# First pair of an attention kernel: projections two at a time, high weight halves first, other staging places for the value weights

## The chip, the core and the metric

The kernel runs on one core of a Trainium2 chip. Its engines are TensorE (PE in the profile), VectorE (DVE), ScalarE (ACT), GpSimd (POOL) and the queue of SyncE (SP), from which nearly all transfers are issued. Each engine runs its own list of instructions in order and waits at semaphores for the others. The metric is the time of one execution on the device in microseconds (us), as the median of the runs.

## What is computed

One block over 16 batches of 64 tokens of width 1024, each with a context of 1024 x 1024. Cut to what matters:

```
q1 = fake_quant(layernorm(x));  q2 = fake_quant(ctx)        # 8-bit codes
x  = x + q1 @ q2                                            # cross product, K = 1024
h  = layernorm(x)
q, k, v = split(h @ qkv_w + qkv_b)                          # 1024 -> 3 x 1024, 32 heads of 32
x  = x + softmax(causal(rope(q) @ rope(k).T * scale)) @ v @ out_w + out_b
x  = x + layernorm(x) @ (W + sum of scaled A,B pairs).T + bias
```

## The kernel before

Two batches are one pair, 128 rows, so there are 8 pairs (i = 0 to 7). A pair takes these steps: its context comes in 16 chunks of 128x1024 (8 per batch), ACT turns each into codes (`quantise`, slot c mod 6 of `code`), and PE multiplies it (`chunk`, two products of 512 columns). The chunks of the first batch (0 to 7) and of the second (8 to 15) add up in the same two banks, `X`. DVE adds them to the rows `xa` (`cross_evac(i, b)`), then normalises (`norm2`), PE turns the result (`x_turn`), ACT makes its high half in f16 (`x_high`) and DVE the low one (`x_low`). Six projections of 512 columns follow (`qkv(i, j)`, banks `D[0]` and `D[1]` in turn), each of 24 products: for each of 8 weight tiles high rows by high weights, high rows by low weights, low rows by high weights (`dense`, L1086 to L1088). DVE rotates the first four (`rotate`), PE turns them (`qk_turn`), the scores follow (`scores`), the softmax on DVE (`softmax_in`: maximum and difference; `softmax_out`: sum and quotient) with the exponent on ACT, the turn of its result (`p_turn`), the values (`values`) and the output projection (`project`; in pair 0 `project_whole` in f32 with the raw weights, L1218). DVE takes it up into `xb` (`out_evac`), on top of a base (`out_base`: `xa` plus the output bias).

Cross products of pair i + 1 are done between the steps of pair i. For that `xa` must hold the rows of pair i + 1: `x_shift(i + 1)` on DVE puts them there after `out_base(i)` has read the old ones. For pair 1 these rows are loaded into `xa` by POOL, which waits for `out_base(0)` (`s_cp`), and `x_shift(1)` waits for that load (`s_x`).

The wait that keeps the two halves of a pair apart in the banks `X` is in `chunk` on PE:

```python
                if c == KC:
                    pe.wait_ge(s_ce, 2 * i + 1)
                pe.wait_ge(s_u8, CHUNKS * i + c + 1)
```

Pair 0 is also when the weights arrive: 24 tiles of 128x1024 in f32 for the projections (0 to 7 query, 8 to 15 key, 16 to 23 value) and 8 for the output (24 to 31). Each lands in a staging place, ACT writes its high half (`weight_hi(j)`, semaphore `s_whi`) and DVE its low half (`weight_lo(j)`, `s_wlo`), and the staging place is free again. Places: query weights lie where the value weights will be (`v_stage`), key weights in the output weights' room (`o_stage`), value weights 16 to 20 in `v_stage` again and 21 to 23 in parts of `at`. Since value weights are staged in the places of value weights, their high half may be written only when an older low half is done.

The order of pair 0 is written out by hand on each engine in `first_pair`, of pair 1 in `next_pair(1, ...)`, which also makes the halves of weights 25 to 31; pairs 2 to 6 are a loop. SP issues in its written order as well: chunks of pair 0, weights 0 to 16, then chunks of pair 1 and weights 17 to 27 in turn. Chunks of pair 1 and later use three slots: the two of `raw` and `lnt`.

## Time and profile before

| | us |
|---|---|
| median of 3 runs | 654.68 (653.92 to 655.34) |
| profiled execution, its time | 654.89 |
| its span | 653.2 |
| PE busy | 610.1 (93%) |
| DVE busy | 447.6 (69%) |
| ACT busy | 297.6 (46%) |

The span is what the instructions cover; 1.7 us of the execution's time lie around it. A busy PE is one that works or whose products are in the pipeline. A timeline row gives start, duration, engine, line, operation, output and inputs, and in brackets the idle time before it with what ended it. A duration has a tail that overlaps the next instruction of the engine, so a step in a chain is better read from start to start. PEclk, the granted clock, is 1.00 at 2.4 GHz and 0.50 at 1.2 GHz.

### The profile page before, as it was taken

What the parts mean: (1) busy time and instruction counts of PE and PEld (TensorE: products, weight loads), DVE (VectorE), ACT (ScalarE), POOL (GpSimd) and SP (SyncE); (2) the same over time, 40 slices, a digit from 0 to 9 for tenths busy, and PEclk for the clock granted to TensorE, in tenths of its full rate; (3) what the DMA queues carried; (4) which work ended last, traced back from release to release, by engine and by line L of the source; (5) the groups of instructions that cost most, each with busy time, mean ns of one, the idle gap of its engine ahead of it and who ended that gap; (6) DMA issues with size and microseconds to landing.
All of it is one profiled execution on the core that took longest, in us unless ns stands there. A gap on an engine that the chain in (4) does not pass through costs nothing.

```text
span 653.2 us, 12686 instructions
## 1 busy us (share of the span) xinstructions
PE 610.1 (93%) x4864; PEld 308.5 (47%) x4864; DVE 447.6 (69%) x895; ACT 297.6 (46%) x374; POOL 11.1 (2%) x20
## 2 busy tenths in 40 slices
PE   1659979998999999999999999999999999899997
PEld 0224444454545555554555455555545554445453
DVE  6599956877755863885487558737674568866761
ACT  5986955773455355455544653544331242201010
POOL 3000000000000000000000000000000000000000
PEclk9769989999999999999999999999999999999999
DMA  8999983861175136416631761363230043113221
GB/s 322 386 388 398 346 314 147 283 231 66 59 265 193 66 144 215 156 64 229 211 115 53 263 221 64 121 232 129 96 131 31 3 149 142 48 66 128 73 89 48
DMA packets 38494, 109.17 MB, mean 167 GB/s; under 512 B 4026, under 2 KB 4282, under 8 KB 38464
## 3 DMA queue, kind: packets, MB, share of 16 engines
q1 hardware_dynamic: 36688, 104.35, 44.7%
q0 software_dynamic: 1344, 4.23, 1.7%
q8 instruction: 20, 0.33, 0.2%
q10 hardware_dynamic: 432, 0.18, 0.1%
q14 instruction: 10, 0.08, 0.0%
HBM read 100.35 MB, written 8.39 MB: 166 GB/s over the span
## 4 chain that ended last, share of the span: by engine, by line
PE 77%; DVE 11%; DMA 5%; issue 3%; SPq 2%; ACT 2%; DVEq 0%; ACTq 0%
PE dense L1086 15%; PE dense L1087 15%; PE dense L1088 14%; PE cross L1108 6%; PE turn L1076 6%; PE dense L1202 4%; PE dense L1203 4%; PE dense L1204 4%; DVE wq L754 3%; PE score L1163 2%; DMA lnt<-in_ctx 2%; SPq L535 2%; DMA wq<-in_ctx 2%; PE score L1189 2%; PE dense L1095 1%
## 5 line engine op out<-in xcount | busy, mean ns | idle before, releaser
L1086 PE MATMUL dense<-wq,xn_h 128*128 128x512 f16 x448 | 170.9, 381 | 5.6 <-DVE at L786 2.1
L1087 PE MATMUL dense<-wq,xn_h 128*128 128x512 f16 x448 | 170.8, 381 | 0.0
L1088 PE MATMUL dense<-wq,xn_l 128*128 128x512 f16 x448 | 170.5, 381 | 0.0
L310 ACT ACTIVATE code<-raw,cst,qc 128x1024 uint8<-128x1024 f32 x77 | 93.8, 1236 | 9.8 <-DMA raw<-in_ctx 8.6
L1108 PE MATMUL cross<-code,q1t 128*128 128x512 f16 x256 | 75.5, 402 | 4.5 <-DVE xa L761 3.5
L1086 PEld LDWEIGHTS dense<-wq,xn_h 128*128 128x128 f16 x448 | 43.9, 98 | 54.3 <-issue 5.9
L1088 PEld LDWEIGHTS dense<-wq,xn_l 128*128 128x128 f16 x448 | 44.0, 98 | 53.4 <-issue 1.0
L1087 PEld LDWEIGHTS dense<-wq,xn_h 128*128 128x128 f16 x448 | 44.0, 98 | 43.0 <-issue 0.5
L783 DVE TENSOR_REDUCE smx<-score 128x8 f32<-128x512 f32 x32 | 22.0, 686 | 49.8 <-PE score L1163 49.8
L310 ACT ACTIVATE code<-lnt,cst,qc 128x1024 uint8<-128x1024 f32 x35 | 43.3, 1238 | 27.4 <-DMA lnt<-in_ctx 20.4
L326 ACT ACTIVATE at<-turn 128x512 f32<-128x512 f32 x32 | 19.0, 595 | 76.2 <-PE turn L1076 76.2
L771 DVE TENSOR_TENSOR rope<-dense,cst 128x512 f32<-128x512 f32 x32 | 22.0, 688 | 36.4 <-PE dense L1088 36.4
L1108 PEld LDWEIGHTS cross<-code,q1t 128*128 128x128 f16 x256 | 25.8, 102 | 40.0 <-issue 7.7
L1202 PE MATMUL dense<-wo,rope 128*128 128x512 f16 x112 | 42.5, 380 | 0.0
L1203 PE MATMUL dense<-wo,rope 128*128 128x512 f16 x112 | 42.4, 379 | 0.0
L1204 PE MATMUL dense<-wo,rope 128*128 128x512 f16 x112 | 42.4, 379 | 0.0
L334 ACT ACTIVATE at<-at 128x512 f32<-128x512 f32 x32 | 20.0, 626 | 40.8 <-DVE at L786 40.8
L760 DVE SCALAR_TENSOR_TENSOR xa<-cross,qc,xa 64x1024 f32<-64x1024 f32 x16 | 20.4, 1274 | 15.6 <-PE cross L1108 15.4
L340 ACT ACTIVATE at<-turn 128x512 f32<-128x512 f32 x32 | 19.0, 595 | 21.6 <-PE turn L1076 21.6
L1086 PE MATMUL dense<-wq,q1t 128*128 128x512 f16 x64 | 24.3, 379 | 0.0
L1087 PE MATMUL dense<-wq,q1t 128*128 128x512 f16 x64 | 24.3, 379 | 0.0
L1088 PE MATMUL dense<-wq,q1t 128*128 128x512 f16 x64 | 24.3, 379 | 0.0
(146 smaller groups left out, 870.2 us busy)
## 6 DMA issues: line engine op xcount, KB each, us to landing
raw<-in_ctx SPq DMA_DIRECT2D x77, 512.0 KB, 4.3
lnt<-in_ctx SPq DMA_DIRECT2D x35, 512.0 KB, 4.3
wq<-in_qkv_w SPq DMA_DIRECT2D x13, 512.0 KB, 11.8
wo<-in_ctx SPq DMA_DIRECT2D x8, 512.0 KB, 8.7
wq<-in_ctx SPq DMA_DIRECT2D x8, 512.0 KB, 11.7
wo<-in_qkv_w SPq DMA_DIRECT2D x8, 512.0 KB, 12.8
x_scratch<-xb SPq DMA_DIRECT2D x8, 512.0 KB, 3.0
wq<-x_scratch SPq DMA_DIRECT2D x8, 512.0 KB, 3.6
```

The costliest lines, as they stand in the source:

```text
L310: act.activation(low_bytes, src, ACT.Identity, scale=qc[:, 1:2], bias=z2).then_inc(s_u8, 1)
L760: link(dve.scalar_tensor_tensor(xa[rows, :], XX[0:SEQ, :], qc[0:SEQ, 2:3], xa[rows, :], ALU.mult, ALU.add))
L771: dve.tensor_tensor(t1, src, cosb, ALU.mult)
L783: link(dve.tensor_reduce(smx[:, g % 2, :], s3, AX.X, ALU.max))
L1076: ins = pe.transpose(bank[:, k * P:(k + 1) * P], src[:, c:c + P], ident)
L1086: pe.matmul(bank[:, :], a_h[:, k, :], w_hi, start=(k == 0 and not started), stop=False)
L1087: pe.matmul(bank[:, :], a_h[:, k, :], w_lo, start=False, stop=False)
L1088: ins = pe.matmul(bank[:, :], a_l[:, k, :], w_hi, start=False, stop=(k == KC - 1))
L1108: ins = pe.matmul(X[n][:, :], lhs, code[:, c % RING, n * NT:(n + 1) * NT], start=(kc == 0), stop=(kc == KC - 1))
L1202: pe.matmul(D[n][:, :], c_h[:, k, :], wo_h[:, k, cols], start=(k == 0), stop=False)
L1203: pe.matmul(D[n][:, :], c_h[:, k, :], wo_l[:, k, cols], start=False, stop=False)
L1204: ins = pe.matmul(D[n][:, :], c_l[:, k, :], wo_h[:, k, cols], start=False, stop=(k == KC - 1))
```

## The change

- **PE, pair 0.** The six projections run in three sets of two banks. Of each set the products with the high weight halves run first for both banks (`high`), then those with the low halves (`low`). `high` waits for `s_whi`, `low` for `s_wlo`. For the first tiles of the first set the products of the high rows run ahead of those of the low rows. The bias products of the first set are ahead of `x_turn`. Chunks of pair 1 start in the low products of the last set, and chunks 7 and 8 stand between the first values and the output projection.
- **Staging.** Value weights 16 to 23 lie in `at`, in both slots of `raw`, in `lnt`, in `at` twice, in `spare` and in the first place of `o_stage`, all outside the places of value weights.
- **SP.** All 24 projection weights and output weights 24 to 27 are issued before the first chunk of pair 1. Chunks 0 to 2 of pair 1 wait for the low halves 17 to 19, which free their slots. Weights 28 to 30 follow chunks 13 to 15.
- **ACT and DVE, pair 0.** Their orders are written anew: ACT makes the high halves up to 23 before any code of pair 1, DVE has `out_base(0)`, `x_shift(1)` and both `cross_evac(1, ...)` behind more of the softmax. The last chunk of pair 0 is coded half on ACT and half on DVE (`last_codes`), and the norm of pair 0 is written in two halves, so that its turn can start on the first.
- **Pair 1.** Low half 31 moves on DVE behind two `softmax_in`.
- ACT's wait before it writes a slot of `code` names, for the first four chunks of a pair, a later product than before.

```diff
@@ staging, SP @@
-            if j < 2 * KC + 5:
-                return v_stage[j - 2 * KC + 3]
             if j < W_QKV:
-                return at_stage[:, j - 2 * KC - 5, :, :]
+                return value_stage[j - 2 * KC]
...
-            for c in range(7):
+            for j in range(W_QKV, W_QKV + 4):
+                load_weight(j)
+            for c in range(13):
                 load_chunk(1, c)
-                load_weight(17 + c)
...
@@ ACT, quantise @@
-                if above(CHUNKS * i + c - RING + 1):
-                    act.wait_ge(s_cmm, CHUNKS * i + c - RING + 1)
+                taken = CHUNKS * i + c - (CHUNKS % RING - 1 if c < CHUNKS % RING else RING - 1)
+                if above(taken):
+                    act.wait_ge(s_cmm, taken)
...
@@ DVE, first_pair @@
-                w(2, 9)
+                w(1, 9)
                 rotate(0, 0)
-                w(9, 13)
                 rotate(0, 1)
-                w(13, 16)
-                out_base(0)
+                w(9, 16)
                 rotate(0, 2)
-                w(16, 20)
                 rotate(0, 3)
-                w(20, 24)
+                w(16, 21)
                 softmax_in(0, 0)
                 softmax_in(0, 1)
-                x_shift(1)
+                w(21, 24)
                 softmax_out(0, 0)
                 softmax_out(0, 1)
-                cross_evac(1, 0)
+                out_base(0)
                 softmax_in(0, 2)
                 softmax_in(0, 3)
+                x_shift(1)
                 softmax_out(0, 2)
                 softmax_out(0, 3)
+                cross_evac(1, 0)
                 cross_evac(1, 1)
...
@@ DVE, next_pair @@
                 cross_evac(i + 1, 0)
-                w(31)
                 if more:
                     row_stats(i + 2, x_early)
                 softmax_in(i, 2)
                 softmax_in(i, 3)
+                w(31)
...
@@ DVE, codes of the last chunk of pair 0 @@
             cross_evac(0, 0)
+            last_codes()
             cross_evac(0, 1)
...
@@ PE, first_pair @@
+                low(2, tiles_due(KC))
+                low(3)
+                started(4)
+                high(4, range(KC), both, high_due(2 * KC), {3: [at(turned, 0, 0), at(qk_turn, 0, 2)], 7: [at(turned, 0, 1), at(qk_turn, 0, 3)]})
+                started(5)
+                high(5, range(KC), both, None, {2: [at(scores, 0, 0)]})
+                low(4, tiles_due(2 * KC), {3: [at(c, 0)], 4: [at(scores, 0, 1), at(c, 1)], 5: [at(c, 2)]})
+                low(5, None, {0: [at(turned, 0, 2), at(p_turn, 0, 0)], 5: [at(p_turn, 0, 1)]})
+                c(3, 4, 5, 6)
                 values_due(0, 0)
-                c(10)
                 values(0, 0)
-                project_whole(0, 0, {0: [at(evacuated, 0, 0), at(p_turn, 0, 2)], 1: [at(c, 11)], 2: [at(evacuated, 0, 1), at(p_turn, 0, 3)], 3: [at(c, 12, 13)]})
-                c(14, 15)
-                project_whole(1, 0, {2: [at(values_due, 0, 1)], 3: [at(values, 0, 1)]})
+                c(7, 8)
+                project_whole(0, 0, {0: [at(c, 9)], 1: [at(evacuated, 0, 0), at(p_turn, 0, 2)], 2: [at(c, 10)], 3: [at(evacuated, 0, 1), at(p_turn, 0, 3)]})
+                project_whole(1, 0, {0: [at(c, 11)], 1: [at(c, 12)], 2: [at(values_due, 0, 1)], 3: [at(values, 0, 1)]})
+                c(13, 14, 15)
```

How the instructions stand shows best at three places; the semaphores that each waits for are in brackets. First DVE in pair 0, around the first `cross_evac` of pair 1 (L760 and L761 before, L763 and L764 after) and the row shift (L738, L730); `smx` and `ssum` are softmax inputs and outputs. Before:

```order
L783 TENSOR_REDUCE smx<-score 128x8 [waits s_sc]
L786 TENSOR_TENSOR at<-score,smx 128x512 [waits s_dv]
L738 TENSOR_SCALAR xa<-xa,rs 128x1024 [waits s_x]
L792 TENSOR_REDUCE ssum<-at 128x8 [waits s_exp,s_xs]
L793 RECIPROCAL ssum<-ssum 128x8 [waits s_dv]
L794 TENSOR_TENSOR at<-at,ssum 128x512 [waits s_dv]
L792 TENSOR_REDUCE ssum<-at 128x8 [waits s_exp]
L793 RECIPROCAL ssum<-ssum 128x8 [waits s_dv]
L794 TENSOR_TENSOR at<-at,ssum 128x512 [waits s_dv]
L760 SCALAR_TENSOR_TENSOR xa<-cross,qc,xa 64x1024 [waits s_cmm]
L761 SCALAR_TENSOR_TENSOR xa<-cross,qc,xa 64x1024 [waits s_dv]
L783 TENSOR_REDUCE smx<-score 128x8 [waits s_sc]
```

After, behind the output base (L719) and the first of two softmax inputs:

```order
L786 TENSOR_REDUCE smx<-score 128x8 [waits s_sc]
L789 TENSOR_TENSOR at<-score,smx 128x512 [waits s_pt,s_dv]
L730 TENSOR_SCALAR xa<-xa,rs 128x1024 [waits s_x]
L795 TENSOR_REDUCE ssum<-at 128x8 [waits s_exp,s_xs]
L796 RECIPROCAL ssum<-ssum 128x8 [waits s_dv]
L797 TENSOR_TENSOR at<-at,ssum 128x512 [waits s_dv]
L795 TENSOR_REDUCE ssum<-at 128x8 [waits s_exp]
L796 RECIPROCAL ssum<-ssum 128x8 [waits s_dv]
L797 TENSOR_TENSOR at<-at,ssum 128x512 [waits s_dv]
L763 SCALAR_TENSOR_TENSOR xa<-cross,qc,xa 64x1024 [waits s_cmm]
L764 SCALAR_TENSOR_TENSOR xa<-cross,qc,xa 64x1024 [waits s_dv]
```

The evacuation of chunks 0 to 7 moved from ahead of the second half's softmax to behind all of it, and the shift with its wait `s_x` went with it.

PE in pair 0 around chunk 8 of pair 1 (`cross` with the wait `s_ce`). Before, in the last products of the sixth projection (L1086 to L1088), with the values of the first half (L1189) and the first product of the output projection (L1218) behind:

```order
L1088 MATMUL dense<-wq,xn_l 128x512
L1108 MATMUL cross<-code,q1t 128x512 [waits s_u8,s_ce]
L1108 MATMUL cross<-code,q1t 128x512
L1086 MATMUL dense<-wq,xn_h 128x512
L1087 MATMUL dense<-wq,xn_h 128x512
L1088 MATMUL dense<-wq,xn_l 128x512
L1108 MATMUL cross<-code,q1t 128x512 [waits s_u8]
L1108 MATMUL cross<-code,q1t 128x512
L1108 MATMUL cross<-code,q1t 128x512 [waits s_sub,s_u8,s_pte,s_v]
L1108 MATMUL cross<-code,q1t 128x512
L1189 MATMUL score<-at 32x64 x32
L1218 MATMUL dense<-wo,rope 128x512 [waits s_w24,s_cl,s_v]
```

After, behind the values of the first half (L1193), with the output projection (L1222) and a turn of the softmax (L1078) behind:

```order
L1193 MATMUL score<-at 32x64 [waits s_sub,s_pte,s_v]
L1193 MATMUL score<-at 32x64 x31
L1112 MATMUL cross<-code,q1t 128x512 [waits s_u8]
L1112 MATMUL cross<-code,q1t 128x512
L1112 MATMUL cross<-code,q1t 128x512 [waits s_u8,s_ce]
L1112 MATMUL cross<-code,q1t 128x512
L1222 MATMUL dense<-wo,rope 128x512 [waits s_w24,s_cl,s_v]
L1112 MATMUL cross<-code,q1t 128x512 [waits s_u8]
L1112 MATMUL cross<-code,q1t 128x512
L1222 MATMUL dense<-wo,rope 128x512 [waits s_w25]
L1078 MATMUL turn<-cst,at 128x128 [waits s_p,s_pte]
L1078 MATMUL turn<-cst,at 128x128 x3
```

Chunk 8 stood ahead of the first values and among projection products; now it stands behind them, and the output projection behind it.

DVE in pair 1, from its `cross_evac` on (L760 and L761 before): low half 31 (`wo<-spare`) and the statistics of the rows after next (from L688). Before:

```order
L760 SCALAR_TENSOR_TENSOR xa<-cross,qc,xa 64x1024 [waits s_cmm]
L761 SCALAR_TENSOR_TENSOR xa<-cross,qc,xa 64x1024 [waits s_dv]
L754 SCALAR_TENSOR_TENSOR wo<-spare,wo 128x1024 [waits s_whi]
L688 BN_STATS st<-at 128x6 [waits s_x]
L689 BN_STATS st<-at 128x6
L690 MEMSET nw 128x1 [waits s_dv]
L691 BN_AGGR mv<-st 128x2
```

After, from the end of those statistics (L702, L703) on, with the low half at L757:

```order
L702 TENSOR_SCALAR ab<-nw,qc 128x1 [waits s_dv]
L703 SCALAR_TENSOR_TENSOR ab<-mv,ab,cst 128x1 [waits s_dv]
L786 TENSOR_REDUCE smx<-score 128x8 [waits s_sc,s_dv]
L789 TENSOR_TENSOR at<-score,smx 128x512 [waits s_pt,s_dv]
L786 TENSOR_REDUCE smx<-score 128x8 [waits s_sc]
L789 TENSOR_TENSOR at<-score,smx 128x512 [waits s_pt,s_dv]
L757 SCALAR_TENSOR_TENSOR wo<-spare,wo 128x1024 [waits s_whi]
L795 TENSOR_REDUCE ssum<-at 128x8 [waits s_exp]
```

The low half went from ahead of the statistics to behind both softmax inputs.

## Rows read from the trace of the kernel before

**Rows 1.** Waits of PE from 180 us on: us in total, times, longest.

```profile
PE cross L1243 <- DVE wq L815: 3.2, 3, 2.2
```

**Rows 2.** Timeline of PE: start us, us, what [idle before it].

```profile
95.05 2.05 PE L1218 MATMUL dense<-wo,rope 128*128 128x512 f32 x2 [4.63 <-issue]
...
106.56 0.86 PE L1189 MATMUL score<-at 64*32 64x64 f32 x64
...
116.42 0.38 PE L1095 MATMUL dense<-bias_t,pick 128*128 128x512 f16 x1 [0.25 <-DVE xb L809]
...
162.69 0.49 PE L1086 MATMUL dense<-wq,xn_h 128*128 128x512 f16 x1 [2.11 <-DVE at L786]
...
180.58 0.38 PE L1095 MATMUL dense<-bias_t,pick 128*128 128x512 f16 x1
...
240.90 0.38 PE L1095 MATMUL dense<-bias_t,pick 128*128 128x512 f16 x1
```

**Rows 3.** Timeline of DVE, pair 0.

```profile
37.26 0.81 DVE L744 TENSOR_SCALAR lnt<-xa,mv,nw 128x1024 f32<-128x1024 f32 x1
...
61.45 1.22 DVE L727 TENSOR_TENSOR xb<-xa,outb 128x1024 f32<-128x1024 f32 x1
62.59 0.68 DVE L771 TENSOR_TENSOR rope<-dense,cst 128x512 f32<-128x512 f32 x1
...
63.52 0.41 DVE L773 TENSOR_TENSOR rope<-dense,cst 128x256 f32<-128x256 f32 x1
...
78.92 0.74 DVE L738 TENSOR_SCALAR xa<-xa,rs 128x1024 f32<-128x1024 f32 x1
79.70 0.69 DVE L792 TENSOR_REDUCE ssum<-at 128x8 f32<-128x512 f32 x1
...
82.82 1.27 DVE L760 SCALAR_TENSOR_TENSOR xa<-cross,qc,xa 64x1024 f32<-64x1024 f32 x1
...
85.45 0.69 DVE L783 TENSOR_REDUCE smx<-score 128x8 f32<-128x512 f32 x1
...
87.50 0.69 DVE L786 TENSOR_TENSOR at<-score,smx 128x512 f32<-128x512 f32 x1
...
103.23 1.28 DVE L760 SCALAR_TENSOR_TENSOR xa<-cross,qc,xa 64x1024 f32<-64x1024 f32 x1 [8.75 <-PE cross L1108]
```

**Rows 4.** Timeline of DVE, pair 1.

```profile
154.52 1.23 DVE L754 SCALAR_TENSOR_TENSOR wo<-spare,wo 128x1024 f16<-128x1024 f32 x1 [3.01 <-ACT wo L293]
...
159.80 0.69 DVE L783 TENSOR_REDUCE smx<-score 128x8 f32<-128x512 f32 x1
```

**Rows 5.** Windows: us, busy PE, PEld, DVE, ACT, POOL, PEclk, DMA share, GB/s.

```profile
95.00:96.00 1.00, 0.95 (x1) 0.50 (x2) 0.00 (x0) 0.00 (x0) 0.00 (x0) 0.50 0.98 344
...
163.00:164.00 1.00, 1.00 (x10) 0.16 (x11) 0.93 (x3) 0.20 (x1) 0.00 (x0) 0.50 0.00 0
```

**Rows 6.** Timeline of ACT, pair 0.

```profile
27.73 2.55 ACT L310 ACTIVATE code<-wq,cst,qc 128x1024 uint8<-128x1024 f32 x2 [0.21 <-DMA wq<-in_ctx]
...
101.14 1.23 ACT L310 ACTIVATE code<-raw,cst,qc 128x1024 uint8<-128x1024 f32 x1
107.45 0.66 ACT L353 ACTIVATE rope<-score 128x256 f32<-128x256 f32 x2 [5.08 <-PE score L1189]
...
108.94 2.37 ACT L310 ACTIVATE code<-raw,cst,qc 128x1024 uint8<-128x1024 f32 x2
```

**Rows 7.** Timeline of POOL, pair 0.

```profile
62.97 0.54 POOL L669 DMA_DIRECT2D xa<-in_x  x1 [24.05 <-DVE xb L727]
```

**Rows 8.** DMA issues, 60 to 100 and 180 to 240 us: KB each, us to landing.

```profile
xa<-in_x POOLq DMA_DIRECT2D x1, 512.0 KB, 6.9
...
at<-in_x POOLq DMA_DIRECT2D x1, 512.0 KB, 5.4
```

**Rows 9.** Line L551, which loads chunks, up to 180 us.

```profile
DMA to landing us min/median/max: 3.0/4.1/6.4
```

**Rows 10.** The page's first line.

```profile
span 653.2 us, 12686 instructions
```

More of the change, by code:

```diff
@@ L505, in _ @@
             a_high(1, 1)
-            for j in range(5):
+            for j in range(6):
                 weight_hi(j)
@@ L540, in load_chunk @@
                         sp.wait_ge(s_u8, CHUNKS * i + c - 2)
-                    elif c == 2:
-                        sp.wait_ge(s_xt, 2)
+                    else:
+                        sp.wait_ge(s_wlo, 2 * KC + 2 + c)
                     sp.dma_start(slots[n], ctx_v[i, c // KC, c % KC, :, :]).then_inc(s_ctx0[c], 16)
@@ L739, in x_shift, with last_codes @@
                 dve.wait_ge(s_xs, i + 1)
+            def last_codes():
+                c = CHUNKS - 1
+                dve.wait_ge(s_ctx0[c], 16)
+                dve.wait_ge(s_cmm, c - RING + 1)
+                low_bytes = code[:, c % RING, :].bitcast(U8T).rearrange("p (a n b) -> p a n b", a=2, b=2)[:, 1, :, 0]
+                dve.tensor_scalar(low_bytes, chunk0_stage(c)[:, 1, :], qc[:, 1:2], z2, ALU.mult, ALU.add).then_inc(s_u8half, 1)
             def norm2(i):
@@ L743, in norm2 @@
                 mean_rstd(xa[:, :], XSC)
-                dve.tensor_scalar(lnt[:, :], xa[:, :], mv[:, 0:1], nw[:, 0:1], ALU.subtract, ALU.mult).then_inc(s_xn, 1)
+                if isinstance(i, int) and i == 0:
+                    dve.tensor_scalar(lnt[:, 0:NT], xa[:, 0:NT], mv[:, 0:1], nw[:, 0:1], ALU.subtract, ALU.mult).then_inc(s_xnhalf, 1)
+                    dve.tensor_scalar(lnt[:, NT:DM], xa[:, NT:DM], mv[:, 0:1], nw[:, 0:1], ALU.subtract, ALU.mult).then_inc(s_xn, 1)
+                else:
+                    dve.tensor_scalar(lnt[:, :], xa[:, :], mv[:, 0:1], nw[:, 0:1], ALU.subtract, ALU.mult).then_inc(s_xn, 1)
             def x_low(i, e):
@@ L965, in _ @@
             cross_evac(0, 0)
+            last_codes()
             cross_evac(0, 1)
             norm2(0)
-            for j in range(2):
-                weight_lo(j)
+            weight_lo(0)
             x_low(0, 0)
@@ L1105, in chunk @@
                 pe.wait_ge(s_u8, CHUNKS * i + c + 1)
+                if isinstance(i, int) and i == 0 and c == CHUNKS - 1:
+                    pe.wait_ge(s_u8half, 1)
                 lhs = q1t[:, kc, b, :, :].rearrange("p h t -> p (h t)")
@@ L1224, in x_turn @@
             def x_turn(i, first=False):
-                pe.wait_ge(s_xn, i + 1)
+                if first:
+                    pe.wait_ge(s_xnhalf, 1)
+                else:
+                    pe.wait_ge(s_xn, i + 1)
                 for e in range(2):
@@ L1266, in evacuated, with started, high, low @@
                 pe.wait_ge(s_pte, 4 * i + g + 1)
+            def started(j):
+                if j > 1:
+                    pe.wait_ge(s_rt, j - 1)
+                bias(D[j % 2], order(0)[j])
+            def high(j, ks, rows, due=None, between={}):
+                n = order(0)[j]
+                for k in ks:
+                    if due:
+                        due(k)
+                    for a in rows:
+                        pe.matmul(D[j % 2][:, :], a[:, k, :], wq_h[:, k, n * NT:(n + 1) * NT], start=False, stop=False)
+                    for step in between.get(k, ()):
+                        step()
+            def low(j, due=None, between={}):
+                n = order(0)[j]
+                for k in range(KC):
+                    if due:
+                        due(k)
+                    ins = pe.matmul(D[j % 2][:, :], xn_h[:, k, :], wq_l[:, k, n * NT:(n + 1) * NT], start=False, stop=(k == KC - 1))
+                    if k == KC - 1:
+                        ins.then_inc(s_qkv, 1)
+                    for step in between.get(k, ()):
+                        step()
+            def high_due(start):
+                return lambda k: pe.wait_ge(s_whi, start + k + 1)
             def first_pair():
@@ new lines, in first_pair @@
+                both = (xn_h, xn_l)
+                high(0, range(5), (xn_h,), rows_high)
+                high(0, range(5), (xn_l,), rows_low)
+                high(0, range(5, KC), both, rows_high)
+                high(1, range(KC), both)
+                low(0, tiles_due(0))
+                low(1)
+                started(2)
+                high(2, range(KC), both, high_due(KC), {7: [at(qk_turn, 0, 0)]})
+                started(3)
+                high(3, range(KC), both, None, {7: [at(qk_turn, 0, 1)]})
```

94 lines of the change are left out of this document (42 added, 52 removed).

## The prediction

> **What bounds the kernel now.** I read the waits of TensorE (PE) first. From 180 us to the end they add up to 4 us [rows 1]: the loop over the pairs keeps PE full, and one pair takes 60.32 us from bias to bias (180.58 to 240.90) [rows 2]. Nothing in the change touches that loop, so its time moves only with the moment at which the loop begins. The two pairs ahead of it do have holes. Pair 0 holds PE up for 4.63 us before the output projection (95.05), and pair 1 takes 64.16 us from 116.42 to 180.58, 3.84 more than a pair of the loop [rows 2]. The reader is to see two chains there. In pair 0 VectorE (DVE) is full from 37.26 to 82.82 with the low weight halves, the rotations and the softmaxes; then the end of the block is set by the last chunk of context of pair 1: its evacuation starts on DVE at 103.23, and PE begins pair 1 13.19 us later [rows 2, 3]. In pair 1 DVE waits 3.01 us for ScalarE (ACT) to give the high half of weight 31 (154.52), so its softmax of the second half starts at 159.80 and PE waits 2.11 us until 162.69 [rows 2, 4]. PE then runs at half clock [rows 5]: the granted clock is 0.50 at 163 to 164, the lower of its levels (1.2 of 2.4 GHz).
>
> **The start.** The last chunk of codes is split, half on ACT, half on DVE. Two whole ones take 2.55 us on ACT, one alone 1.23 [rows 6], and half is some 0.6: a gain of 0.6, less about 0.05 for the norm written in two halves (0.81 whole, at 37.26 [rows 3]). So 0.55. The new instruction on DVE stands where DVE waits for the same chunk anyway, so it is free. Bounds: 0 (DVE's half takes as long as the whole) to 0.65.
>
> **The projections two at a time.** PE no longer waits for low halves before it uses high ones. But DVE's work stays: 24 low halves, 4 rotations, 2 low row halves, 2 softmax inputs, 2 outputs. DVE is the chain here, so I sum its time by difference. The second softmax output ends at 82.82 now (the next instruction's start) [rows 3]. Taken out ahead of it are the output base (1.14 us, from 61.45 to 62.59) and the row shift (0.78 from 78.92 to 79.70) [rows 3]; the start gives 0.55. I add 0.5 for new small waits (for the rows' high halves, for low products behind the last low half of a set): 82.82 - 1.14 - 0.78 - 0.55 + 0.5 = 80.9. Bounds 80.4 and 82. PE then has one turn and two products left and is done with the projections at about 82. Weight transfers now come in one row, so ACT's high halves keep ahead of DVE; SP's queue issues all 24 before the first chunk of pair 1, whose slot holds value weight 17 until its low half is made. That is 12.7 us before DVE's 80.9 (three low halves, two softmax inputs, three low halves, two outputs), at 68.2. The first chunk's codes then come at about 73 instead of 57, but PE asks for them only at 75. That costs nothing by itself.
>
> At one place a rule speaks against pairing. Here DVE frees a bank while PE runs the eight low products of the other one. The Trainium skill (Perfetto Trace Analysis, Optimizing Tensor Performance, Matmuls) says that independent groups should rotate through different banks so that emptying one overlaps the next group's products; two groups that end together overlap less. By that rule alone two rotations would stand open; by the program they are covered. That rule is priced as a rival below.
>
> **What is late next: chunk 8 of pair 1.** This is the term that decides. Chunks 0 to 7 and 8 to 15 of a pair go to the same banks, so chunk 8 waits until DVE has evacuated chunks 0 to 7 (its `s_ce` wait in PE's order). Before, that evacuation ran at 82.82, ahead of the second half's softmax [rows 3], and PE came to chunk 8 later. After, it is behind the output base, two softmax inputs, the row shift and two softmax outputs. And the shift reads rows that POOL loads into `xa`, issued when the output base is done. So:
> - output base 80.9 to 82.05; POOL issues 0.35 us after its end (61.45 + 1.22 to 62.97 [rows 3, 7]): 82.4.
> - landing: 6.9 us for this load now, on full transfer engines; 5.4 for the like load of pair 2; the shortest chunk load takes 3.0 [rows 8, 9]. I take 5.4, since few chunks are in flight then: 87.8. DVE has come to the shift at 84.7 (two softmax inputs, 2.65: 85.45 to 87.50 + 0.69, less the overlap with what follows [rows 3]) and idles 3.1 us.
> - shift 0.78, two softmax outputs 3.12 (79.70 to 82.82), evacuation 2.63 (82.82 to 85.45) [rows 3]: 94.3. Chunk 8 runs at 94.4.
>
> PE has nothing else. ACT gives the codes of chunks 5 and 6 behind its last copy of the projections (82.6 + 2.37 = 85.0), so the values of the first half end at 86.3; copy (0.55), codes of chunk 7 (1.23) and two products (0.43) come to 88.5. Then chunk 8 heads PE's queue, and the whole output projection stands behind it. So PE idles about 6 us, where it idled 4.63 before. From chunk 8 to the end of the second half's values PE has the same work as now from 95.05: four products of the first projection and four of the second, two turns, five chunks, one set of values. That took 106.56 + 0.86 - 95.05 = 12.4 us, the half-clock stretch after the hole in it (granted clock 0.50 at 95 to 96) [rows 2, 5]. Since the hole is longer now, I take the same 12.4: 106.8. At full clock it would be 10.9.
>
> Then comes a piece that wasn't in series before: ACT's order puts the context copy (0.66 long, 0.55 in series) and chunks 14 and 15 (2.37) behind those values, and from the last code to the evacuation it takes 0.86 (101.14 + 1.23 to 103.23) [rows 3, 6]. 106.8 + 0.55 + 2.37 + 0.86 = 110.6 against 103.23: 7.4 us later. Behind it stands the same DVE chain of 13.19 us (evacuation, norm, next rows' statistics, low rows, output). PE's remaining work, one half projection of 3.5, the turn and another of 3.5, fits under it even if half of it runs at half clock. So pair 1 starts 7.4 us later. Bounds: the load lands in 3.0 (-2.4) or 6.9 (+1.5), the clock costs 0 (-1.5) or twice (+1.5).
>
> **Pair 1.** Low half 31 moves on DVE from ahead of the statistics to behind the two softmax inputs. The statistics then start right after the evacuation, at 151.5 in this trace's time (154.52 - 3.01) and take the same 4.1, and the inputs then wait for nothing but the scores, which PE ends at about 155.9; now they start at 159.80 [rows 4]. They end at 158.6, before PE asks at 160.4. Hole and half clock go; the pair then takes what a loop pair takes: -3.84, of which I count 3.7, since PE's turn of the next rows comes only 0.2 us after DVE has them. Bounds -3.0 and -3.84. The new ring waits (`s_cmm`) of ACT are met long before; the other pairs are unchanged.
>
> **Sum.** On the profiled execution (654.89 us, its span 653.2 [rows 10]): +7.4 - 3.7 = +3.7, 658.6. The median of the runs is 654.68, 0.2 below it, so the forecast is 658.4.
>
> **The rivals.**
> - Same: the rows land in 3.0 us and PE keeps its full clock. 7.4 - 2.4 - 1.5 - 3.7 = -0.2: 654.5. For it: transfers are thin at that point. Against it: both 512 KB loads by POOL read here took 5.4 or more, and after a hole of 4.63 the clock was halved [rows 2, 5, 8]. Chance 0.13, taken to be within 0.2% (1.3 us, about what a measurement of this kernel can tell from no change).
> - Faster: the change does what it says, because the evacuation is not what chunk 8 waits for (DVE far earlier than I sum). Then ACT's codes bind: chunk 8's at 89.3 (copy after the values at 86.9, two chunks 2.37), 10.9 of PE and 3.8 of ACT and PE, 104.0: +0.8 - 3.7 = -2.9, 651.8. It decides once the evacuation ends before 89.3, 5.0 earlier than I get. Against it: DVE has no idle time to lose. Chance 0.09.
> - Open rotations: the time from first to last reading of a bank, 1.34 of a rotation (62.59 to 63.52 + 0.41 [rows 3]), comes into the chain once (ahead of the scores) and finds 0.15 of slack: +1.2, 659.6. Chance 0.12. It is the rule above as a mechanism.
> - Pair 1 keeps its hole, since ACT gives weight 31 late or the row turn becomes the wait: +7.4, 662.1. Chance 0.08.
> - My case: 0.58.
>
> **How the numbers follow.** The range takes in the load's and the clock's bounds: 654.6 to 661.2. What's left out is most of the faster case and the last one. Faster by over 0.2% 0.09, within 0.2% 0.13, slower 0.78.
>
> **What would show it.** Right: the first evacuation of pair 1 on DVE at about 91.7 with a wait for a transfer of about 3 us before the shift; PE idle before chunk 8 for about 6 us; granted clock 0.5 behind it; last evacuation at about 110.6; pair 1 from bias to bias 60.4 to 60.5. Wrong: chunk 8 runs before 90, or the wait before it names ACT's codes; pair 1 still over 63; projections that end after 84, since then DVE's chain is missummed.

## The result: slower by 0.8%, and where the time stands

The changed kernel takes 660.26 us (median of four runs, 659.31 to 661.05) against 654.30 for the kernel before, measured beside it: a ratio of 1.0079, 95% interval 1.0052 to 1.0107. The forecast was 658.4, range 654.6 to 661.2. The profiled execution took 659.62 us, and its page begins (before: [rows 10]):

```profile
span 658.0 us, 12691 instructions
```

The waits of PE from 180 us on are the old one and nothing else [rows 1], so the loop over the pairs is unchanged:

```profile
PE cross L1252 <- DVE wq L818: 3.2, 3, 2.2
```

The timeline of PE (start us, us, what, idle before it) shows both halves of the result; the rows answer to [rows 2]:

```profile
90.47 1.03 PE L1112 MATMUL cross<-code,q1t 128*128 128x512 f16 x2 [1.88 <-ACT code L313]
95.48 1.03 PE L1112 MATMUL cross<-code,q1t 128*128 128x512 f16 x2 [3.98 <-DVE xa L764]
96.31 1.91 PE L1222 MATMUL dense<-wo,rope 128*128 128x512 f32 x2
...
108.20 0.86 PE L1193 MATMUL score<-at 64*32 64x64 f32 x64
...
125.89 0.38 PE L1097 MATMUL dense<-bias_t,pick 128*128 128x512 f16 x1 [1.50 <-DVE xb L812]
...
186.30 0.38 PE L1097 MATMUL dense<-bias_t,pick 128*128 128x512 f16 x1
...
246.62 0.38 PE L1097 MATMUL dense<-bias_t,pick 128*128 128x512 f16 x1
```

Pair 1 begins at 125.89 instead of 116.42, 9.47 later. It then takes 60.41 us (to 186.30) instead of 64.16, 3.75 less, practically a pair of the loop (60.32). So the loop begins 5.72 later. The span grew by 4.8 only: from pair 3's bias to the end it is 411.4 us here and 412.3 before, of which 0.8 is a wait at the start of the feed-forward part that this trace lacks. That tail is not touched by any kernel of this study, and it spread from 411.4 to 414.1 over the thirteen traces. In the six with a tail of 413.0 or more the granted clock fell, once, between 550 and 575 us (to 0.66 to 0.82 in the lowest stretch of 5 us); in the seven with 412.5 or less it stayed 1.00 from 240 us on. So I compare traces at the biases, and whole kernels by medians.

What PE waited for at 95.48 stands on DVE; the rows answer to [rows 3], and the pairing's first half did what it was to do (DVE's softmax output ends at 82.25, and no low half is waited for on DVE):

```profile
37.61 0.55 DVE L744 TENSOR_SCALAR lnt<-xa,mv,nw 128x512 f32<-128x512 f32 x1
38.08 0.54 DVE L745 TENSOR_SCALAR lnt<-xa,mv,nw 128x512 f32<-128x512 f32 x1
...
82.25 1.22 DVE L719 TENSOR_TENSOR xb<-xa,outb 128x1024 f32<-128x1024 f32 x1
...
88.92 0.75 DVE L730 TENSOR_SCALAR xa<-xa,rs 128x1024 f32<-128x1024 f32 x1 [2.80 <-DMA xa<-in_x]
...
92.83 1.27 DVE L763 SCALAR_TENSOR_TENSOR xa<-cross,qc,xa 64x1024 f32<-64x1024 f32 x1
...
112.71 1.28 DVE L763 SCALAR_TENSOR_TENSOR xa<-cross,qc,xa 64x1024 f32<-64x1024 f32 x1 [17.29 <-PE cross L1112]
```

And POOL, which issues the load (before: 62.97 [rows 7]):

```profile
83.76 0.53 POOL L661 DMA_DIRECT2D xa<-in_x  x1 [44.31 <-DVE xb L719]
```

Two engines' orders meet here. On ACT's timeline the codes of pair 1 wait for their context five times, 8.7 us in all; the two longest waits are shown, before the first chunk (whose codes came at 55.65 before) and before chunk 10. The last two chunks stand behind the copy of the second half's values, as forecast (before: [rows 6]):

```profile
73.28 1.24 ACT L313 ACTIVATE code<-raw,cst,qc 128x1024 uint8<-128x1024 f32 x1 [3.19 <-DMA raw<-in_ctx]
...
96.35 1.24 ACT L313 ACTIVATE code<-raw,cst,qc 128x1024 uint8<-128x1024 f32 x1 [3.10 <-DMA raw<-in_ctx]
...
109.10 0.66 ACT L356 ACTIVATE rope<-score 128x256 f32<-128x256 f32 x2 [2.23 <-PE score L1193]
109.64 1.24 ACT L313 ACTIVATE code<-lnt,cst,qc 128x1024 uint8<-128x1024 f32 x1
110.78 1.24 ACT L313 ACTIVATE code<-raw,cst,qc 128x1024 uint8<-128x1024 f32 x1
```

The windows (us, busy PE, PEld, DVE, ACT, POOL, PEclk, DMA share, GB/s) show what the two holes of PE did to its clock (before: [rows 5]):

```profile
85.00:90.00 5.00, 2.32 (x68) 1.17 (x68) 2.13 (x4) 4.22 (x7) 0.00 (x0) 0.73 0.83 292
90.00:95.00 5.00, 1.03 (x2) 0.13 (x2) 4.83 (x8) 2.89 (x3) 0.53 (x1) 0.50 0.85 301
95.00:100.00 5.00, 4.52 (x8) 1.98 (x9) 0.42 (x1) 2.37 (x2) 0.00 (x0) 0.50 0.73 269
100.00:105.00 5.00, 5.00 (x19) 2.50 (x18) 0.00 (x0) 1.59 (x3) 0.00 (x0) 0.90 0.92 333
```

### The profile page after: what moved, and what is told of

It is laid out like the page before. It is cut to its first block, busy times and chain, and to the rows that moved or that the text cites. A ratio compares the mean times of both kernels' runs of the same rounds, so it can differ in the third digit from the quotient of the medians.

```text
span 658.0 us, 12691 instructions
## 1 busy us (share of the span) xinstructions
PE 610.8 (93%) x4864; PEld 307.9 (47%) x4864; DVE 448.2 (68%) x897; ACT 298.3 (45%) x374; POOL 11.1 (2%) x20
## 4 chain that ended last, share of the span: by engine, by line
PE 81%; DVE 12%; DMA 3%; SPq 2%; issue 1%; ACT 1%; DVEq 0%; ACTq 0%
PE dense L1088 15%; PE dense L1090 15%; PE dense L1089 15%; PE cross L1112 7%; PE turn L1078 6%; DVE wq L757 4%; PE dense L1206 4%; PE dense L1207 4%; PE dense L1208 4%; PE score L1167 3%; SPq L525 2%; DMA wq<-in_ctx 2%; PE score L1193 2%; PE dense L1097 1%; PE dense L1222 1%
## 5 line engine op out<-in xcount | busy, mean ns | idle before, releaser
L1088 PE MATMUL dense<-wq,xn_h 128*128 128x512 f16 x400 | 151.8, 380 | 0.0
L1090 PE MATMUL dense<-wq,xn_l 128*128 128x512 f16 x400 | 151.6, 379 | 0.0
L1089 PE MATMUL dense<-wq,xn_h 128*128 128x512 f16 x400 | 151.6, 379 | 0.0
L1112 PE MATMUL cross<-code,q1t 128*128 128x512 f16 x256 | 77.5, 407 | 14.6 <-DVE xa L764 7.4
L1090 PEld LDWEIGHTS dense<-wq,xn_l 128*128 128x128 f16 x400 | 39.1, 98 | 47.2
L1088 PEld LDWEIGHTS dense<-wq,xn_h 128*128 128x128 f16 x400 | 39.1, 98 | 39.7 <-issue 0.6
L1089 PEld LDWEIGHTS dense<-wq,xn_h 128*128 128x128 f16 x400 | 39.1, 98 | 38.9
L1206 PE MATMUL dense<-wo,rope 128*128 128x512 f16 x112 | 42.5, 380 | 0.0
L763 DVE SCALAR_TENSOR_TENSOR xa<-cross,qc,xa 64x1024 f32<-64x1024 f32 x16 | 20.4, 1273 | 18.4 <-PE cross L1112 18.3
L1078 PE MATMUL turn<-cst,lnt 128*128 128x128 f32 x128 | 17.6, 283 | 9.8 <-DVE lnt L744 6.0
L1088 PE MATMUL dense<-wq,q1t 128*128 128x512 f16 x64 | 24.3, 379 | 0.0
L1089 PE MATMUL dense<-wq,q1t 128*128 128x512 f16 x64 | 24.3, 379 | 0.0
```

Of the source, the lines that this page charges most:

```text
L1078: ins = pe.transpose(bank[:, k * P:(k + 1) * P], src[:, c:c + P], ident)
L1088: pe.matmul(bank[:, :], a_h[:, k, :], w_hi, start=(k == 0 and not started), stop=False)
L1089: pe.matmul(bank[:, :], a_h[:, k, :], w_lo, start=False, stop=False)
L1090: ins = pe.matmul(bank[:, :], a_l[:, k, :], w_hi, start=False, stop=(k == KC - 1))
L1112: ins = pe.matmul(X[n][:, :], lhs, code[:, c % RING, n * NT:(n + 1) * NT], start=(kc == 0), stop=(kc == KC - 1))
L1206: pe.matmul(D[n][:, :], c_h[:, k, :], wo_h[:, k, cols], start=(k == 0), stop=False)
```

## The experiments

My theory after the result: the loss is made in pair 0, by chunk 8 of pair 1 standing ahead of the projection while the evacuation of `xa` waits for a load; the gain is made in pair 1, by low half 31 alone. The main rival for the loss was the supply of codes (ACT's order, or the context loads, whose slots now hold value weights until DVE has split them).

The profiled executions differ in the moment at which the last chunk of pair 0 lands, from 28.91 to 30.86 us, though no edit touches the loads up to it. Where two traces are compared, that part of a difference is named.

**Low half 31.** First the gain by itself: the kernel before with this edit and nothing else.

```diff
                 cross_evac(i + 1, 0)
-                w(31)
                 if more:
                     row_stats(i + 2, x_early)
                 softmax_in(i, 2)
                 softmax_in(i, 3)
+                w(31)
```

> The kernel before with one edit of the change: in pair 1 low half 31 stands on DVE behind two softmax inputs. Theory: DVE's statistics start 4 us earlier, PE's hole of 2.11 us in pair 1 and the half clock behind it go, pair 1 takes 60.3 to 60.5 us from bias to bias in place of 64.16, and the kernel 3.7 us less than before (-0.57%). Rival: pair 1 got shorter in the changed kernel only because its start lay otherwise against the transfers; then this edit alone gives 0 to 1 us.

Measured: 651.56 us (12 runs) against 655.52, ratio 0.9949 (0.9930 to 0.9968), -3.3 us by the ratio and -4.0 by the medians. Pair 1 is 60.44 us long there:

```profile
116.24 0.38 PE L1095 MATMUL dense<-bias_t,pick 128*128 128x512 f16 x1 [0.24 <-DVE xb L809]
...
176.68 0.38 PE L1095 MATMUL dense<-bias_t,pick 128*128 128x512 f16 x1
```

The same edit backwards, on the changed kernel:

> The changed kernel with that one edit undone: low half 31 ahead of the statistics again. Theory: pair 1 takes about 64.1 us again, the kernel 3.7 us more than the changed one, so some 9.3 more than before (+1.4%). Rival: as the changed kernel, since its weight 31 lands at another moment.

Measured: 662.90 (6 runs), ratio 1.0116 (1.0089 to 1.0144), 2.4 us over the changed kernel's 1.0079, less than the 3.7 expected; the two intervals touch, so the trace decides. Pair 1 is 64.0 us long again (124.56 to 188.56), and the old wait is back in PE's list of waits:

```profile
PE dense L1088 <- DVE at L789: 2.1, 1, 2.1
```

So the 3.6 to 3.7 us of pair 1 come from this one line and don't depend on the rest. The first of the two beats both kernels.

**The load into `xa`.** The output base moves ahead of low halves 16 to 20, so that POOL issues the load early.

```diff
                 rotate(0, 3)
+                out_base(0)
                 w(16, 21)
...
                 softmax_out(0, 1)
-                out_base(0)
                 softmax_in(0, 2)
```

> The changed kernel with the output base of pair 0 earlier on DVE, ahead of low halves 16 to 20, so that the load of the next rows is issued some 15 us earlier. DVE's wait of 2.80 us before the row shift goes in any case. If that load is what makes chunk 8 of pair 1 late, chunk 8 runs 2.8 us earlier and the kernel takes 2.8 less than the changed one. My theory after its trace: the evacuation can't start before the products of chunk 7 (90.47 + 1.03), whose codes hang on ACT's chain behind the first half's softmax, and that chain gets 1.14 us longer by the base: chunk 8 only 0.2 to 1.5 us earlier, the kernel 0 to 1.5 less than the changed one.

Measured: 660.25 (6 runs), ratio 1.0074 (1.0048 to 1.0099): no gain. On DVE's timeline the shift no longer waits, and the next instruction does, for ACT:

```profile
85.59 0.74 DVE L730 TENSOR_SCALAR xa<-xa,rs 128x1024 f32<-128x1024 f32 x1
88.63 0.69 DVE L795 TENSOR_REDUCE ssum<-at 128x8 f32<-128x512 f32 x1 [2.30 <-ACT at L337]
...
91.99 1.28 DVE L763 SCALAR_TENSOR_TENSOR xa<-cross,qc,xa 64x1024 f32<-64x1024 f32 x1
```

The exponents stand behind the codes of chunks 5 and 6 in ACT's order. The load's wait was real, but another stood right behind it, and the evacuation came only 0.8 earlier (91.99 for 92.83), 0.5 of it because the last chunk of pair 0 landed that much earlier. What was left was lost again behind the last evacuation, which came at 112.01 for 112.71. PE then idled 3.75 us in both traces, but here its turn and half projection behind that hole ran at half clock, and pair 1 began at 126.06 for 125.89:

```profile
119.16 1.97 PE L1078 MATMUL turn<-cst,lnt 128*128 128x128 f32 x8 [3.75 <-DVE lnt L747]
```

**Chunk 8 behind the projection's first half.** On the changed kernel, PE's order only:

```diff
-                c(7, 8)
-                project_whole(0, 0, {0: [at(c, 9)], 1: [at(evacuated, 0, 0), at(p_turn, 0, 2)], 2: [at(c, 10)], 3: [at(evacuated, 0, 1), at(p_turn, 0, 3)]})
-                project_whole(1, 0, {0: [at(c, 11)], 1: [at(c, 12)], 2: [at(values_due, 0, 1)], 3: [at(values, 0, 1)]})
+                c(7)
+                project_whole(0, 0, {1: [at(evacuated, 0, 0), at(p_turn, 0, 2)], 3: [at(evacuated, 0, 1), at(p_turn, 0, 3), at(c, 8, 9)]})
+                project_whole(1, 0, {0: [at(c, 10, 11)], 1: [at(c, 12)], 2: [at(values_due, 0, 1)], 3: [at(values, 0, 1)]})
```

> The changed kernel with only PE's order changed: the first half of the first output projection stands ahead of chunks 8 and 9, which come behind it with 10 and 11. Theory (chunk 8 at the head of PE's queue holds up work that doesn't need it): PE's wait for the evacuation, 3.98 us, vanishes behind the projection, the half clock is paid under it, the values of the second half end 5 to 6 us earlier than at 109.06, and the kernel takes about 5.5 less than the changed one, so about as long as before. Rival (the codes of chunks 10 to 12, whose transfers and ring are late since the slots held weights, bind): less than 2 us less, with waits of PE for ACT's codes in the place.

Measured: 657.76 (12 runs), ratio 1.0032 (1.0012 to 1.0053), half of what I expected. The wait for DVE is gone, and the last evacuation comes at 110.49, 2.2 earlier, 0.5 of that from the start. All that PE still waits for there is codes, 7.8 us against 6.2 in the changed kernel:

```profile
PE cross L1112 <- ACT code L313: 7.8, 7, 2.5
```

But all but 1.9 us of these waits lie ahead of the projection (93.60). From there to the end of the second half's values (106.84) PE waited for nothing; it was slow, at half clock until about 98.4:

```profile
90.00:95.00 5.00, 3.12 (x68) 1.79 (x51) 3.54 (x6) 4.04 (x5) 0.09 (x1) 0.50 0.84 298
95.00:100.00 5.00, 5.00 (x13) 2.42 (x12) 1.41 (x2) 2.11 (x2) 0.00 (x0) 0.66 0.80 261
```

So this run doesn't show by itself that the supply of codes was the limit. The next one, at full clock, does.

Both edits together:

> The changed kernel with both earlier edits together: the output base ahead of the low halves 16 to 20 (so the load into xa starts early), and chunk 8 behind the first projection tile. Theory now: what holds the pair back is the supply of codes for chunks 8 to 15 (each load waits for its slot, each code for the scalar engine), so the base's place matters no more than before: within 0.7 of the kernel with chunk 8 later alone (657.8), 657.1 to 658.5. Rival: the load into xa is the second chain and was only covered by the first: then its wait of 2.2 us goes as well, 655.6.

Measured: 658.79 (4 runs), ratio 1.0066 (1.0040 to 1.0092), nothing gained over chunk 8 alone: the intervals of the two overlap, and counted from DVE's first low half, pair 1 begins 1.7 us earlier than in the changed kernel with chunk 8 alone and 1.4 earlier here. This trace is the clearest one. PE's clock is 1.00 from 75 to 105, the projection starts at 92.19, the second half's values end at 104.7, 4.4 us sooner than in the changed kernel. Still the last evacuation is at 111.29. On ACT's timeline the last codes are what is late:

```profile
103.33 1.24 ACT L313 ACTIVATE code<-raw,cst,qc 128x1024 uint8<-128x1024 f32 x1 [1.82 <-DMA raw<-in_ctx]
104.72 0.66 ACT L356 ACTIVATE rope<-score 128x256 f32<-128x256 f32 x2
106.30 1.24 ACT L313 ACTIVATE code<-lnt,cst,qc 128x1024 uint8<-128x1024 f32 x1 [0.93 <-DMA lnt<-in_ctx]
108.92 1.24 ACT L313 ACTIVATE code<-raw,cst,qc 128x1024 uint8<-128x1024 f32 x1 [1.38 <-DMA raw<-in_ctx]
```

From the first (75.26) to the last (108.92), fifteen intervals take 33.66 us, 2.24 for each chunk: three slots, each refilled only when its codes are made. A chunk's codes take ACT 1.24. From 66 to 116 us ACT sat idle for context 16.1 us in all, 5.2 of it before the first codes, 8.5 between the first and the last, and 2.5 before those of pair 2:

```profile
its engine sat idle before it (us, times) until:
  DMA raw<-in_ctx: 14.9, 9
  DMA lnt<-in_ctx: 1.2, 2
```

**The supply of context taken away.** Two kernels make pair 1's codes from a tile that has long been in place, so pair 1's output is wrong; all instructions and loads stay. Not shown are waits on SP and DVE that keep a place from being written before its last loads have landed.

```diff
                     if isinstance(i, int) and i == 1:
-                        act.wait_ge(s_ctx0[c], 32)
+                        src = outb[:, :].rearrange("p (a n) -> p a n", a=2)
+                        act.wait_ge(s_outb, 16)
...
                     if c >= 3:
-                        sp.wait_ge(s_u8, CHUNKS * i + c - 2)
+                        sp.wait_ge(s_ctx0[c - 3], 32)
```

On the kernel with both edits:

> The same edit of the codes' source (pair 1's codes are made from the output bias tile, so pair 1's output is wrong), on the kernel with the output base early and chunk 8 later. Theory: what is left there is the supply of context chunks, whose first codes start at 75.3 us and whose last are made at 108.9, 2.24 us for each of fifteen, at slots that the value weights held till then. With the data at hand the last evacuation comes at about 105.0 and not 111.3 (projection from 90.0, 11.2 us to the end of the second half's values, two chunks of codes and a chunk's product), so 658.8 - 6.3 = 652.5, 651.5 to 653.8. Rival (the order of the instructions on the scalar engine, which is unchanged, holds the last codes back): within 1 us of 658.8.

Measured: 655.09 (10 runs), ratio 1.0013 (1.0004 to 1.0023), against 1.0066: 0.5%, 3.5 us where I expected 6.3. In the trace the last evacuation is at 105.04, the 105.0 of the sum, and pair 1 begins at 118.24 and not 124.45:

```profile
105.04 1.28 DVE L768 SCALAR_TENSOR_TENSOR xa<-cross,qc,xa 64x1024 f32<-64x1024 f32 x1 [11.70 <-PE cross L1117]
```

0.8 of those 6.2 us is the start: the last chunk of pair 0 landed at 28.99 and not 29.78. So the supply is worth 5.4 at pair 1, with the clock 1.00 in both traces from 75 to 105. 1.6 are taken back in the tail (413.0 against 411.4), where this trace has the fall of the clock and the other has not. Most of what is left between traces and medians is that the traced execution here took 1.4 less than the median of its kernel (653.67), the other one 0.5 less. And on the changed kernel itself:

> The changed kernel, with ScalarE making pair 1's sixteen chunks of codes from the output bias tile (128x1024 f32, long in place) in place of the context that is loaded: the codes of pair 1 are wrong, and so is the output of pair 1; all the loads are still made, each behind the one before it in its slot. This takes the wait for the context out of the scalar engine's order and leaves every instruction. Theory: two chains run side by side in the changed kernel, the codes and the load into xa; with the codes at hand the second is left alone. The load still lands at 88.9, the first evacuation stays at 92.8, chunk 8 at 95.5 and the last evacuation at 112.0 to 112.7: 659.5 to 660.3. Rival (the supply of codes alone sets the end): 3 us or more are gained, 657 or less.

Measured: 661.76 (4 runs), ratio 1.0106 (1.0085 to 1.0127): no gain, perhaps a loss. With the codes at hand the transfer engines were busier (share 0.98 from 85 to 90, for 0.83), and the load into `xa`, issued at 83.04, landed only at 91.1, after 8 us:

```profile
91.14 0.75 DVE L733 TENSOR_SCALAR xa<-xa,rs 128x1024 f32<-128x1024 f32 x1 [5.75 <-DMA xa<-in_x]
```

PE then waited 8.06 us for the evacuation. So this edit made the other chain longer, by the 3 us that the load took more (8.1 for 5.1), and pair 1 began at 126.93. As an estimate from these rows, without that delay it would have begun at about 123.9, or 124.7 if the start had been the changed kernel's. Against the changed kernel's 125.89, and with the start evened out, the load's chain alone taken away gives 1.4 us, the supply alone about 1.2, and both together 6.8. The two chains stand side by side, and each hides most of what the other is worth.

**Where the supply is lost.** Value weights 16 and 17 take the first two slots, so the loads of chunks 0 and 1 wait for one low half fewer (on the kernel with both edits):

```diff
-        value_stage = [at_stage[:, 1, :, :]] + [s.rearrange("p (a n) -> p a n", a=2) for s in slots] + [at_stage[:, 0, :, :], at_stage[:, 2, :, :],
+        value_stage = [s.rearrange("p (a n) -> p a n", a=2) for s in slots[:2]] + [at_stage[:, 1, :, :], slots[2].rearrange("p (a n) -> p a n", a=2)] + [at_stage[:, 0, :, :], at_stage[:, 2, :, :],
...
-                        sp.wait_ge(s_wlo, 2 * KC + 2 + c)
+                        sp.wait_ge(s_wlo, 2 * KC + (1, 2, 4)[c])
```

> As the run with the base early and chunk 8 later, and value weights 16 and 17 in the first two chunk slots (18 in the A^T stage, 19 in the third slot as before), so that the loads of chunks 0 and 1 of pair 1 wait for one low half fewer each. Theory (late chunk loads hold the codes back): the first codes, 73.3 to 74.7 us so far, start some 1.15 us earlier, the refills behind them too, and the kernel gains 0.8 to 1.2. Rival (the scalar engine's order or the DMA queue's rate holds them back): the first codes come earlier and the last evacuation doesn't, within 0.3 of the other run.

Measured: 658.48 (8 runs, 655.31 to 659.41), ratio 1.0050 (1.0029 to 1.0070) against 1.0066 (1.0040 to 1.0092). In the trace the first codes come at 73.16 (75.26) and the last evacuation at 108.58 (111.29); the whole trace is 0.9 earlier from the start, so 1.2 and 1.8 are left. In the trace that is the direction and the size, but the intervals of the times overlap, so this run by itself decides nothing.

**The start.** The changed kernel with whole codes of chunk 15 and whole normalised rows:

> The changed kernel with the split of chunk 15's codes and of the first normalised rows undone (both whole again, as in the kernel before); all else as changed. My forecast's term: the start was 0.55 us earlier by these splits, so undoing them gives 660.3 + 0.55 = 660.8. What the trace after says instead: chunk 15 landed at 29.82 against 29.03 before, its 512-wide codes took 0.82 and not 0.6, and the first low half began at 38.53 against 38.0, so the splits gave nothing that can be seen; then the time stays 660.3 within 0.4, or falls a little, to 659.9.

Measured: 661.98 (6 runs), ratio 1.0105 (1.0084 to 1.0125), where the changed kernel had 1.0079 (1.0052 to 1.0107). The direction is that of a worth of the splits, but the intervals overlap. In this trace the last chunk landed at 30.86, a microsecond later than in the changed kernel's, and PE multiplied it at half clock; a single pair of traces says little here.

Counted from that landing the traces agree. Of the four kernels without the splits, the three that don't have that half clock make ACT's first high part of the rows 10.26 to 10.27 us behind it and start DVE's first low half 8.94 to 8.96 behind it; eight of the nine kernels with the splits take 9.54 to 9.56 and 8.71 to 8.72. So the splits give the rows' high part 0.7 us and DVE 0.25.

**Towards a faster kernel.** The kernel before with low half 31 moved still idles 3.95 us before the projection, since ACT has two exponents, an evacuation and two chunks of codes ahead of the context copy. Only ACT's order changes:

```diff
-                q(11)
                 exponent(0, 2)
-                q(12)
+                q(11)
                 exponent(0, 3)
-                v_evac(0, 1)
-                q(13)
                 c_whole(0)
+                q(12)
+                v_evac(0, 1)
                 p_evac(0, 2)
-                q(14)
+                q(13)
                 p_evac(0, 3)
-                q(15)
+                q(14)
+                q(15)
                 c_whole(1)
```

> The kernel before, with low half 31 moved behind the two softmax inputs (as in the run with that part alone) and ScalarE's order in the first pair's second half changed: exponents 2 and 3 around codes 11, then at once the context rows of the first half, and codes 12 to 15 between the later evacuations. In the run with low half 31 alone, the values of the first half end at 90.7 and ScalarE turns to them only at 93.9, since two exponents, an evacuation and two chunks of codes stand ahead; TensorE is idle 3.95 us there. Theory: the context rows run at 90.75, the projection starts at 91.4 and not 94.6, all that follows moves with it: 651.6 - 3.2 = 648.4. Rival: the last evacuation follows the codes of chunk 15, whose loads and codes (1.24 us each, five of them) don't come earlier: 650.5 to 651.6.

Measured: 647.47 (6 runs) against 654.57 (expected: 648.4), ratio 0.9898 (0.9875 to 0.9921), with the next one the fastest of the study. PE's timeline has the hole cut to 0.80, and its clock is 1.00 from 90 to 100:

```profile
92.13 1.10 PE L1218 MATMUL dense<-wo,rope 128*128 128x512 f32 x2 [0.80 <-issue]
...
113.02 0.38 PE L1095 MATMUL dense<-bias_t,pick 128*128 128x512 f16 x1 [0.24 <-DVE xb L809]
```

With the changed kernel's start added (the splits, and low half 1 behind the first rows' low part):

> The kernel before with three edits: low half 31 behind the two softmax inputs, ScalarE's order of the first pair's second half as in the run with that order, and, taken from the changed kernel, the split of chunk 15's codes and of the first normalised rows over two engines and two pieces, with one low half and not two ahead of the first rows' low part. Over the run with the order (647.5): the first rows' high part came at 38.45 to 39.4 us (mean 38.9 of six) in the kernels with the split, and at 39.3 to 41.5 (mean 40.2 of four) in those without: -0.5 to -1.3, so 646.2 to 647.0. Rival (the low halves or weights that follow are late instead, so the first projections wait): no gain, 647.5.

Measured: 648.01 (4 runs), ratio 0.9900 (0.9883 to 0.9916): the rival, no gain. The rows are there at 39.21 (40.23 without, 0.3 of it the landing), but pair 1 begins at 112.97 (113.02): PE's waits for low halves grew from 2.3 to 3.4 us.

```profile
PE dense L1101 <- DVE wq L769: 3.4, 9, 0.7
```

In the old order each projection still follows DVE, tile by tile, and DVE gets no further by it: its third low half starts at 42.5 in both traces.

## Why the prediction was right, point by point

**Start, -0.55.** Within its bounds, and too large: 0.25. The low halves began 0.5 later than before (38.53 for 37.99), but chunk 15 had landed 0.8 later. Before (the chain, then DVE's timeline), and after:

```profile
29.03 1.25 ACT code L310
37.99 1.22 DVE L754 SCALAR_TENSOR_TENSOR wq<-wq 128x1024 f16<-128x1024 f32 x1
```

```profile
29.82 0.55 DVE L738 TENSOR_SCALAR code<-wq,qc,cst 128x512 uint8<-128x512 f32 x1 [5.77 <-DMA wq<-in_ctx]
38.53 1.22 DVE L757 SCALAR_TENSOR_TENSOR wq<-wq 128x1024 f16<-128x1024 f32 x1
```

ACT's half took 0.82 and not 0.6, and the norm in two halves 0.92 (37.61 to 38.53) for 0.73 whole, so it cost 0.2 and not 0.05.

**DVE's sum, 80.9.** It ended at 82.25, 1.3 late and just over the upper bound of 82. 0.8 of this is chance, the later landing; 0.3 is the smaller worth of the splits; the other terms held within 0.3.

**The load into `xa`.** Issued at 83.76, landed after 5.1 (taken: 5.4), evacuation at 92.83 (91.7), chunk 8 at 95.48 (94.4): the offset of 1.1 to 1.3 is DVE's. The idle time was not one hole of 6 us. Chunk 7 ran at 90.47, not 88.5: codes 5 and 6 were ready only at 85.7 and 86.8, behind chunk 4's, which had waited 1.33 for its context, and the projections' last copies. 1.88 of idle time stands before it and 3.98 behind.

**"That costs nothing by itself".** This step was wrong, though it moved no number much: the first codes at 73 (73.28) were foreseen, and I held them harmless because PE asks for them at 75. With three slots a late start was a late end: in the run with both edits the last codes came at 108.92, fifteen times 2.24 us after the first at 75.26. I had priced the faster rival by ACT's time alone (651.8, last evacuation at 104.0). With the evacuation's wait gone (the two edits together) it was 658.8 and 111.29, with the supply gone too 655.1 and 105.04. So what I gave as one chain was two, and by the traces (for the supply by an estimate) either one alone held pair 1 back by all but 1.2 to 1.4 us of what both did. The time came out near the forecast since the chain that I did price was about as long as the one that I had called harmless.

**From chunk 8 to the values, 12.4.** It took 13.6 (95.48 to 109.06). The clock was 0.50 up to 100 and 0.90 from 100 to 105; half clock had begun before chunk 8, and chunk 7 between two holes did not bring it back. Within the bound of +1.5.

**The end in series, and pair 1's start.** 109.06 to 112.71 is 3.65 for the 3.78 of the sum; from the evacuation to pair 1 13.18 for 13.19. Last evacuation 9.5 later than before, forecast 7.4; the +2.1 is chunk 8's 1.1 and the clock's 1.2, less 0.1. That PE's remaining work fits under DVE's chain at half clock was a near thing: in the run with the output base early it took 0.9 us more than fits.

**Pair 1, -3.7.** It was -3.75, and -3.72 in the run with that part alone. (PE's asking time was 160.6 and not 160.4, 162.69 less its wait of 2.11; nothing hangs on it.) The last softmax input ends at 168.10; less the 9.47 by which the pair began later, that is the 158.6 of the forecast. It is low half 31 that stands behind it now (before: [rows 4]), on DVE:

```profile
167.41 0.69 DVE L789 TENSOR_TENSOR at<-score,smx 128x512 f32<-128x512 f32 x1
168.01 1.21 DVE L757 SCALAR_TENSOR_TENSOR wo<-spare,wo 128x1024 f16<-128x1024 f32 x1
```

The new ring waits cost nothing: up to 200 us ACT waits once for PE before codes, 1.2 us, as in the kernel before.

**Sum.** +9.47 - 3.75 = +5.72 at the loop, +5.2 by the ratio, +6.0 by the medians, forecast +3.7. Of the 2.0 missed at the loop 0.8 is the landing of chunk 15 in this execution and 1.2 the clock. The open rotations' 1.2 didn't appear: in the changed kernel no wait of PE up to 180 us names a rotation, and one of 0.7 us a low half. The Trainium skill (Perfetto Trace Analysis, Optimizing Tensor Performance, Matmuls) advises rotating independent groups through banks, so that emptying one overlaps the next group's products. This trace shows no loss from sets of two that end eight products apart. The same-time rival failed on both its conditions, landing 5.1 and clock 0.50.

## What to carry to other kernels

Price every part of a bundle apart: here one moved line gives 3.7 us, and the rest of the change costs 8.7 (9.5 in the trace, 0.8 of it chance). When an operation is moved behind another in an engine's order, follow what its completion starts, a load on another queue and who reads it, and ask the same of each buffer that is lent out: here a refill chain of three slots that started 18 us later also ended later, though its first item had slack. If removing one wait gives little, remove the second chain too before calling the first harmless; two nearly equal chains make each other look cheap. And before two traces are compared, look whether they start alike and whether the clock was the same in both.

## What the runs showed of the hardware

- The conversion to bytes in every second place took 0.82 us on ACT for 128x512 and 1.24 for 128x1024; on DVE the half took 0.55. Splitting it in halves over the two engines saved 0.4 of 1.24.
- The same 512 KB load by POOL landed after 5.1 us in the changed kernel (the transfer engines' share was 0.83 from 85 to 90) and after 8.1 with the codes at hand (0.98 there); before it took 6.9 [rows 8]. In the four kernels that issue it at 68 to 69 it took 3.4 to 3.9; in the one with both edits the share was 0.01 from 68 to 70.
- A few products between two holes didn't restore TensorE's clock: 0.50 from 90 to 100, with 1.03 us of work in the first five of these; where PE idled 0.8 before the projection it stayed 1.00. The holes alone don't tell the clock: PE idled 1.88 us before chunk 7 in the changed kernel and in the one with both edits, and from 88 to 92 the clock was 0.50 in the first, where it had begun to fall at 87, and 1.00 in the second.
- The last chunk of pair 0 landed between 28.91 and 30.86 us over the thirteen traces, with the same loads ahead of it. Behind pair 3, where the program is the same, they spread by 2.7 us, and the longest six are those in which the clock fell there.
